# Unread products in front of TensorE's data waits, and a third part turned earlier, in a graph network kernel

## The chip, the cores and the metric

The kernel runs on one core of a Trainium2 chip. The metric is the device time of one execution in microseconds. TensorE is PE in the profile (PEld is its weight load), VectorE is DVE, ScalarE is ACT, GpSimd is POOL and SyncE, which only issues transfers here, is SP.

## The reference

A graph of 50,000 nodes and 50,000 edges, the edges sorted by their destination, goes through four message passing layers; each ends with a layer norm over the 160 features of a node (64 scalars, and 32 vectors of three components). Cut to what matters:

```python
x = _layernorm(x + _L0_gnn_ref(x, node_vec1, edge_attr_3, edge_attr_64, src, dst, ...))  # attention
x = _layernorm(x + _L1_gnn_ref(x, node_vec1, edge_attr_16, edge_attr_4, src, dst, ...))  # mean
x = _layernorm(x + _L2_gnn_ref(x, node_vec1, edge_attr_4, edge_attr_8, ..., src, dst, 16))
x = _layernorm(x + _L3_gnn_ref(x, node_vec1, src, dst, edge_attr_4, edge_attr_64, ...))

# each layer, in short
h = silu(edge_scalars @ fc_w1); w = h @ fc_w2              # weights of an edge
m = combine(w, (x @ lin1)[src], edge_attr)                 # messages, scalars and vectors
agg = segment_sum(m, dst)                                  # sums of a node
y = x @ sc + agg @ lin2                                    # and gates of each layer's own
```

Layer 0 has a two-layer radial network with layer norms, attention logits with a softmax over a node's edges, and a feed-forward part behind it.

## The kernel before

Everything is float32. Nodes and edges are padded to 98 chunks of 512, a chunk being 4 tiles of 128. The program is a row of stages, each over all 98 chunks, with tables in DRAM between them: setup, node_pre (98 to 497 us), edge_logits (600 to 2096), edge_softmax, node_first (2620 to 3858), and then edge_layer and node_layer for the layers 1, 2 and 3.

Within a stage every engine has a program of its own, written with `pipeline(engine, chunks, [(stage, delay), ...])`: in round r the engine executes, in the order of the list, each stage for chunk r - delay. That list is the order of the work. Engines wait on each other only by semaphores (`wait_ge`). A product on PE has two kinds of wait: for its data (an earlier engine's result), and for its bank in PSUM (the reader of the last product in it must be done). A round is one chunk, so all engines of a stage have the same mean round.

The names that matter:

- `turn` (L391) transposes five 128x128 blocks into a bank pair, `mix` (L397, L400) multiplies the turned rows by a layer's weights in ten products.
- edge_logits: PE's stages in order are values of r = 0, roots (`r2`, `r1`), `h1`, `h2`, values of r = 1, two variances, `messages_t` (12 transposes, L1353), weights of r = 0 (L1360), `logits` (4 transposes, L1380), weights of r = 1 (L1360). ACT copies or evaluates each result out of PSUM. POOL issues eight gathers a chunk and takes powers (L1279). DVE makes the messages.
- node_first: PE runs `hidden` (L1759 to L1764), turn and mix of sums, projection (L1739 to L1744), turns and `outputs` (L1777 to L1782).
- edge_layer: PE runs `hidden` (L473), turns of the message parts (L487; two parts in layers 1 and 2, three in layer 3), `sums` (L510), `weights` (L497) and `linear` (L522 to L525). In layer 3 the third part's turn stands between weights and linear. ACT copies (L557 turned, L562 rows, L544 radial).
- node_layer: PE runs `front` (turn of the loaded rows), and for layers 1 and 2 `turn_out`, `back` (mix of the skip part), `mix_out`; for layer 3 only front and back. SP loads indices and rows and stores the normalised rows. POOL gathers the sums (L718) and takes a power (L767). DVE runs `before` (L967 to L973 in layer 3) and `combine` (L1011 to L1018, statistics L739 to L755).

In node layer 3 the banks of `back` alternate (`sc_s` is 2048 + 1024 * slot), but its product also waits for DVE's `combine` two chunks back:

```python
pe.wait_ge(xt_sb.sem, xt_sb.after(s.g + 1))
pe.wait_ge(sum_step.sem, sum_step.after((s.g - 1 + with_e) * sum_steps - with_e * (sum_steps - read)))
pe.wait_ge(pre_step.sem, pre_step.after((s.g - 1) * pre_steps))
```

## Time and profile before

| | us |
|---|---|
| median of 3 runs | 8838.66 (8814.75 to 8842.85) |
| the profiled execution | 8821.47 |
| its span | 8819.7 |
| PE busy | 6072.5 (69%) |
| PE weight load busy | 5115.7 (58%) |
| DVE busy | 6244.2 (71%) |
| ACT busy | 4194.7 (48%) |
| POOL busy | 4731.4 (54%) |

The mean granted TensorE clock is 0.822 of full speed. The profile's page gives the shares over the whole span; since the stages have different limits, they are read stage by stage from the trace. In a timeline a line shows start, duration, engine, line of the program, operation, operands, and in brackets the engine's idle time before it and what ended it. A line of the waits gives an engine and its line, what released it, the sum in us, how many times and the longest.

### The profile page before, as it was taken

The numbers are of one execution on the slowest core, as the hardware profiler recorded it, in microseconds if no ns is written. First come the engines' busy times: TensorE is split into PE (matmuls) and PEld (weight loads), VectorE is DVE, ScalarE is ACT, GpSimd is POOL, SyncE is SP. The second block draws the span as 40 slices with busy tenths as digits, with TensorE's granted clock in tenths as the row PEclk, the third lists the DMA queues.
The fourth block names the chain that finished last, engine by engine and source line by source line (L and its number), as shares of the span: only waits on it lengthen the run. The fifth ranks groups of instructions, "written<-read, shape, count | busy, mean of one in ns | idle before, by whom it ended". The sixth has DMA issues, their size and how long they took to land. (4 is left out here: it accounts for less than half of the span.)

```text
span 8819.7 us, 169625 instructions
## 1 busy us (share of the span) xinstructions
PE 6072.5 (69%) x36496; PEld 5115.7 (58%) x36496; DVE 6244.2 (71%) x20178; ACT 4194.7 (48%) x10003; POOL 4731.4 (54%) x4424
## 2 busy tenths in 40 slices
PE   3767777776657777777776666777666678884444
PEld 3555555555556666656665655666566567774443
DVE  6967777777658887866565775666688878785666
ACT  2544444443325555544444775444466645553333
POOL 3456666664445555545444554445466544445666
PEclk9977777776559999988888887889788899996666
DMA  6732222224753333334444665444466544443444
GB/s 185 242 119 75 75 76 75 77 71 133 205 168 105 108 110 103 106 92 120 116 117 131 198 196 158 116 116 120 122 178 179 172 120 129 128 122 115 128 128 124
DMA packets 774197, 1137.24 MB, mean 129 GB/s; under 512 B 322032, under 2 KB 410038, under 8 KB 773648
## 3 DMA queue, kind: packets, MB, share of 16 engines
q1 hardware_dynamic: 591952, 831.36, 30.2%
q0 software_dynamic: 182144, 304.74, 15.4%
q8 instruction: 37, 0.61, 0.0%
q14 instruction: 64, 0.52, 0.0%
HBM read 667.03 MB, written 472.87 MB: 129 GB/s over the span
## 5 line engine op out<-in xcount | busy, mean ns | idle before, releaser
L718 POOL DMA_INDIRECT agg<-seg_rows,node_idx x1568 | 1530.1, 976 | 1137.2 <-issue 924.4
L457 POOL DMA_INDIRECT erow<-e_rows,ids x1176 | 1220.0, 1037 | 1282.4 <-issue 1176.6
L397 PE MATMUL banks<-w_all,xt 128*128 128x128 f32 (+1 forms) x2352 | 559.7, 375 | 939.8 <-DVE stats L755 424.4
L397 PEld LDWEIGHTS banks<-w_all,xt 128*128 128x128 f32 x2352 | 439.2, 251 | 1027.9 <-issue 999.5
L767 POOL TENSOR_TENSOR stats<-stats,power 128x4 f32<-128x4 f32 (+1 forms) x392 | 524.8, 1339 | 544.6 <-DVE stats L755 341.9
L655 POOL DMA_INDIRECT row_of_dram<-where x392 | 431.7, 1101 | 559.0 <-DMA where<-place_dram 417.9
L487 PE MATMUL banks<-w_all,mid 128*128 128x128 f32 (+1 forms) x2744 | 457.9, 293 | 395.4 <-ACT hid_p L538 355.0
L400 PE MATMUL banks<-w_all,xt 128*128 128x128 f32 x3528 | 658.5, 339 | 0.0
L487 PEld LDWEIGHTS banks<-w_all,mid 128*128 128x128 f32 (+1 forms) x2744 | 327.7, 146 | 524.0 <-ACT hid_p L538 415.7
L400 PEld LDWEIGHTS banks<-w_all,xt 128*128 128x128 f32 x3528 | 620.9, 254 | 0.0
L544 ACT ACTIVATE radial<-banks 128x768 f32<-128x768 f32 (+1 forms) x294 | 248.6, 846 | 650.1 <-PE banks L497 362.1
L523 PE MATMUL banks<-w_all,turned 128*128 128x97 f32 (+1 forms) x2352 | 502.4, 297 | 43.0 <-issue 33.2
L1272 POOL DMA_INDIRECT y<-dst_table,edge_idx x392 | 439.8, 1122 | 119.5 <-issue 119.5
L557 ACT ACTIVATE turned<-banks 128x512 f32<-128x512 f32 (+1 forms) x686 | 409.5, 599 | 195.7 <-PE banks L487 101.6
L562 ACT ACTIVATE rows<-banks 128x772 f32<-128x772 f32 (+1 forms) x294 | 250.0, 850 | 493.7 <-PE banks L525 293.1
L1272 POOL DMA_INDIRECT work<-src_table,edge_idx x392 | 415.7, 1061 | 112.1 <-issue 112.1
L525 PE MATMUL banks<-w_all,turned 128*128 128x96 f32 x2352 | 459.9, 278 | 0.0
L510 PE MATMUL banks<-rows,segs 128*128 128x161 f32 (+1 forms) x2352 | 451.9, 342 | 3.2 <-DVE rows L618 3.2
L359 DVE TENSOR_TENSOR mid<-radial,erow 128x256 f32<-128x256 f32 x294 | 125.6, 427 | 436.0 <-issue 184.6
L523 PEld LDWEIGHTS banks<-w_all,turned 128*128 128x128 f32 x2352 | 375.7, 201 | 99.5 <-issue 89.8
L582 DVE TENSOR_TENSOR segs<-dst_row,ids 128x512 f32<-128x512 int32 x294 | 202.8, 690 | 323.6 <-remote 117.2
L785 ACT ACTIVATE xo<-y,stats 128x64 f32<-128x64 f32 (+1 forms) x1200 | 428.4, 445 | 0.0
(282 smaller groups left out, 18272.0 us busy)
## 6 DMA issues: line engine op xcount, KB each, us to landing
x_rows<-xo SPq DMA_DIRECT2D x294, 324.0 KB
xin<-x_rows SPq DMA_DIRECT2D x294, 324.0 KB
e_rows<-ets SPq DMA_DIRECT2D x294, 322.0 KB
dst_row<-in_dst_flat SPq DMA_DIRECT2D x294, 256.0 KB
xin<-in_x SPq DMA_DIRECT2D x196, 324.0 KB
seg_rows<-res SPq DMA_DIRECT2D x196, 322.0 KB
seg_rows<-res SPq DMA_DIRECT2D x98, 384.0 KB
seg_rows<-res SPq DMA_DIRECT2D x98, 338.0 KB
```

The source lines that it names most:

```text
L397: pe.matmul(flat[:, to + k * cols:to + (k + 1) * cols], of[:, k * P:(k + 1) * P], W(w_s), start=True, stop=True)
L400: last = pe.matmul(flat[:, to + 2 * cols + k * P:to + 2 * cols + (k + 1) * P], of[:, (2 + k) * P:(3 + k) * P], W(w_v), start=True, stop=True)
L457: pool.indirect_dma_start(erow[s.quad][:, t, 0:EROW], None, table, bass.IndirectOffsetOnAxis(ids[s.quad][:, t:t + 1], 0),).then_inc(edges_ ...
L487: last = pe.transpose(psum[0:n, b, t * P:(t + 1) * P], mid[s.slot][:, t, k * P:k * P + n], ident)
L510: last = pe.matmul(tiled(6, cols)[:, t], segs[s.quad][:, t, :], rows[s.slot][:, t, 0:cols], start=True, stop=True)
L523: pe.matmul(to[:, t, 0:v_at + C1], mid_t[:, 0, cut], W(f"la{layer}"), start=not crossed, stop=True, skip_group_check=crossed)
L525: last = pe.matmul(to[:, t, v_at + C1:cols + C1], mid_t[:, 1, cut], W(f"lb{layer}"), start=not crossed, stop=True, skip_group_check=crossed)
L655: pool.indirect_dma_start(row_of_dram, bass.IndirectOffsetOnAxis(where[b][:, at + t:at + t + 1], 0), where[b][:, at + TILES + t:at + TILES ...
L718: pool.indirect_dma_start(agg[s.quad][:, t, 0:SUM_COLS[layer]], None, seg_rows[layer], bass.IndirectOffsetOnAxis(node_idx[s.slot][:, t, 0: ...
L767: pool.tensor_tensor(st[:, at + n:at + 2 * n], st[:, at:at + n], power[:, 0:n], ALU.pow) \
L785: last = act.activation(to, of if at == 0 else of.rearrange("p (i c) -> p i c", i=3), ACT.Identity, bias=st[:, 40 + t:41 + t], scale=st[:, ...
L1272: pool.indirect_dma_start(to[s.slot][:, t, :], None, table, bass.IndirectOffsetOnAxis(idx[s.slot][:, first + t:first + t + 1], 0),).then_i ...
```

## The change

A helper `spare(pe, b, times)` issues products of the identity with 512 columns of the weights into bank b, which nobody reads. It is put between the wait for the bank and the wait for the data, so in several places the two waits change their order. In the logits: two in `messages_t`, two before the weights of r = 0, one before the values of r = 0, one in `logits` (six a round). In node_first: one in `hidden`, one in `outputs`. In edge layers 1 and 2: one in `linear`. In node layers 1 and 2: two in `turn_out`, two in `mix_out`. In node layer 3: five in `back`, where the wait for `sum_step` is dropped. That makes 588 + 196 + 196 + 784 + 490 = 2254 such products.

In edge layer 3 the third part is turned (PE) and copied (ACT) right after the other two. In edge layers the bank's wait of `linear` comes first. In node layers SP issues its stores one round earlier.

```diff
+        def spare(pe, b, times):
+
+            for _ in range(times):
+                pe.matmul(bank(b), ident, w_all[:, 0:512], start=True, stop=True)
...
                     def linear(s):
 
+                        pe.wait_ge(linear_sb.sem, linear_sb.after(s.g))
+                        if not crossed:
+                            spare(pe, 4, 1)
                         pe.wait_ge(part_sb.sem, part_sb.after(parts * (s.g + 1)))
-                        pe.wait_ge(linear_sb.sem, linear_sb.after(s.g))
...
-                        (hidden, 0), (lambda s: turn_part(s, 0), 2), (lambda s: turn_part(s, 1), 2), (sums, 4), (weights, 0),
-                        *[(lambda s: turn_part(s, 2), 2)][:parts - 2], (linear, 2)])
+                        (hidden, 0), (lambda s: turn_part(s, 0), 2), (lambda s: turn_part(s, 1), 2),
+                        *[(lambda s: turn_part(s, 2), 2)][:parts - 2], (sums, 4), (weights, 0), (linear, 2)])
...
-                        (hidden, 0), (lambda s: copy_part(s, 0), 2), (lambda s: copy_part(s, 1), 2), (weights, 0),
-                        *[(lambda s: copy_part(s, 2), 2)][:parts - 2], (sums, 4), *[(wrap, 0)][:crossed], (linear, 2)])
+                        (hidden, 0), (lambda s: copy_part(s, 0), 2), (lambda s: copy_part(s, 1), 2),
+                        *[(lambda s: copy_part(s, 2), 2)][:parts - 2], (weights, 0), (sums, 4), *[(wrap, 0)][:crossed], (linear, 2)])
...
-        def turn_out(pe, s, to):
+        def turn_out(pe, s, to, times=0):
             precompute(pe, norm_sb.after(s.g + 1), xt3_sb.after(s.g))
             pe.wait_ge(ready.sem, 1)
+            pe.wait_ge(xt3_sb.sem, xt3_sb.after(s.g))
+            spare(pe, to // 512, times)
             pe.wait_ge(norm_sb.sem, norm_sb.after(s.g + 1))
-            pe.wait_ge(xt3_sb.sem, xt3_sb.after(s.g))
...
-        def mix_out(pe, s, layer, to):
+        def mix_out(pe, s, layer, to, times=0):
             precompute(pe, xt3_sb.after(s.g + 1), ets_sb.after(s.g))
             pe.wait_ge(ready.sem, 1)
+            pe.wait_ge(ets_sb.sem, ets_sb.after(s.g))
+            spare(pe, to // 512, times)
             pe.wait_ge(xt3_sb.sem, xt3_sb.after(s.g + 1))
-            pe.wait_ge(ets_sb.sem, ets_sb.after(s.g))
...
-                        pipeline(sp, chunks, [loads, (lambda s: store_nodes(sp, s, x_rows[layer + 1]), 6),
-                                              (lambda s: store_e(sp, s, layer + 1), 7)])
+                        pipeline(sp, chunks, [loads, (lambda s: store_nodes(sp, s, x_rows[layer + 1]), 5),
+                                              (lambda s: store_e(sp, s, layer + 1), 6)])
                     else:
-                        pipeline(sp, chunks, [loads, (store_out, 6)])
+                        pipeline(sp, chunks, [loads, (store_out, 5)])
...
                     def back(s):
 
+                        if not with_e:
+                            pe.wait_ge(pre_step.sem, pre_step.after((s.g - 1) * pre_steps))
+                            spare(pe, sc_s(s) // 512, 5)
                         pe.wait_ge(xt_sb.sem, xt_sb.after(s.g + 1))
-                        pe.wait_ge(sum_step.sem, sum_step.after((s.g - 1 + with_e) * sum_steps - with_e * (sum_steps - read)))
+                        if with_e:
+                            pe.wait_ge(sum_step.sem, sum_step.after(s.g * sum_steps - (sum_steps - read)))
...
-                        stages = [(front, 0), (lambda s: turn_out(pe, s, TURN2), 4), (back, 0),
-                                  (lambda s: mix_out(pe, s, layer + 1, 3072), 4)]
+                        stages = [(front, 0), (lambda s: turn_out(pe, s, TURN2, 2), 4), (back, 0),
+                                  (lambda s: mix_out(pe, s, layer + 1, 3072, 2), 4)]
...
                     def messages_t(s):
+                        pe.wait_ge(agg_sb.sem, agg_sb.after(3 * s.g - 1))
+                        spare(pe, 0, 2)
                         pe.wait_ge(mid_step.sem, mid_step.after((s.g + 1) * steps))
...
                     def weights(s, r):
+                        pe.wait_ge(w_sb.sem, w_sb.after(2 * s.g + r))
                         if r == 0:
+                            spare(pe, 7, 2)
                             pe.wait_ge(silu2_sb.sem, silu2_sb.after(s.g + 1))
-                        pe.wait_ge(w_sb.sem, w_sb.after(2 * s.g + r))
...
                     def values(s, r):
+                        pe.wait_ge(val_sb.sem, val_sb.after(2 * s.g + r))
                         if r == 0:
+                            spare(pe, 3, 1)
                             pe.wait_ge(agg_sb.sem, agg_sb.after(3 * s.g + 3))
-                        pe.wait_ge(val_sb.sem, val_sb.after(2 * s.g + r))
...
                     def logits(s):
                         precompute(pe, leaky_step.after(s.g * leaky_steps + 3), logit_sb.after(s.g))
                         pe.wait_ge(ready.sem, 1)
+                        pe.wait_ge(logit_sb.sem, logit_sb.after(s.g))
+                        spare(pe, 2, 1)
                         pe.wait_ge(leaky_step.sem, leaky_step.after(s.g * leaky_steps + 3))
-                        pe.wait_ge(logit_sb.sem, logit_sb.after(s.g))
...
                     def hidden(s):
 
+                        pe.wait_ge(hidden_step.sem, hidden_step.after(s.g * hidden_steps))
+                        spare(pe, 4, 1)
                         pe.wait_ge(xt2_sb.sem, xt2_sb.after(s.g + 1))
-                        pe.wait_ge(hidden_step.sem, hidden_step.after(s.g * hidden_steps))
...
                         pe.wait_ge(ets_sb.sem, ets_sb.after(s.g - 2))
+                        pe.wait_ge(mid_step.sem, read)
+                        spare(pe, 2, 1)
                         pe.wait_ge(gate_sb.sem, gate_sb.after(s.g + 1))
                         pe.wait_ge(hidden_step.sem, hidden_step.after((s.g + 1) * hidden_steps))
-                        pe.wait_ge(mid_step.sem, read)
```

## Rows read from the trace of the kernel before

**Rows 1.** Windows by stage: length, busy PE, PEld, DVE, ACT, POOL, PEclk, DMA, GB/s.
```profile
600.00:2096.00 1496.00, 1125.22 (x5663) 840.14 (x5664) 1083.94 (x2352) 675.22 (x1879) 966.86 (x835) 0.75 0.28 74
2620.00:3858.00 1238.00, 948.88 (x6764) 795.30 (x6764) 1019.10 (x4529) 657.04 (x1701) 637.57 (x574) 0.96 0.37 105
3905.00:4711.00 806.00, 612.15 (x4014) 525.70 (x4016) 486.85 (x1257) 343.74 (x574) 396.37 (x391) 0.85 0.44 116
4753.00:5421.00 668.00, 427.05 (x2848) 390.89 (x2849) 497.86 (x2033) 464.48 (x1321) 370.55 (x387) 0.85 0.66 193
5450.00:6250.00 800.00, 597.08 (x4008) 511.97 (x4009) 485.56 (x1256) 344.34 (x575) 398.22 (x391) 0.88 0.44 115
6295.00:7032.00 737.00, 461.03 (x2829) 431.87 (x2829) 639.20 (x2791) 490.01 (x1411) 479.49 (x482) 0.80 0.61 174
7064.00:7931.00 867.00, 709.09 (x5162) 601.41 (x5158) 688.98 (x1646) 449.04 (x767) 420.11 (x390) 0.98 0.45 125
7981.00:8805.00 824.00, 379.31 (x1450) 344.21 (x1450) 504.84 (x1635) 283.58 (x671) 531.49 (x482) 0.62 0.44 127
```

**Rows 2.** Timeline of node layer 3, 8400 to 8420 us.
```profile
8401.35 1.64 PE L397 MATMUL banks<-w_all,xt 128*128 128x192 f32 x4 [4.81 <-DVE stats L755]
...
8404.07 1.27 PE L391 MATMUL banks<-w_all,xin 128*128 128x128 f32 x5
...
8409.25 1.02 POOL L718 DMA_INDIRECT agg<-seg_rows,node_idx  x1 [2.02 <-issue]
...
8409.84 1.64 PE L397 MATMUL banks<-w_all,xt 128*128 128x192 f32 x4 [4.50 <-DVE stats L755]
...
8412.80 0.56 DVE L967 TENSOR_TENSOR aux<-banks,agg 128x384 f32<-128x384 f32 x1 [3.03 <-PE banks L400]
...
8414.05 1.66 POOL L767 TENSOR_TENSOR stats<-stats,power 128x4 f32<-128x4 f32 x1
```

**Rows 3.** Waits, 8200 to 8600 us (node layer 3).
```profile
ACT work L901 <- DMA out<-work: 163.2, 47, 4.0
```

**Rows 4.** Timeline of edge layer 3, 7500 to 7520 us.
```profile
7504.59 0.92 ACT L544 ACTIVATE radial<-banks 128x896 f32<-128x896 f32 x1 [1.77 <-PE banks L497]
7505.41 0.58 ACT L557 ACTIVATE turned<-banks 96x512 f32<-96x512 f32 x1
...
7506.12 0.46 PE L522 MATMUL banks<-w_all,turned 96*128 96x96 f32 x2 [1.10 <-ACT turned L557]
```

**Rows 5.** Timeline of the logits, 1466 to 1481 us, PE and DVE.
```profile
1469.41 1.01 PE L1360 MATMUL banks<-w_all,u 128*128 128x448 f32 x2 [1.27 <-ACT u L1410]
...
1471.71 1.02 PE L1360 MATMUL banks<-w_all,u 128*128 128x448 f32 x2 [0.84 <-DVE radial L1517]
...
1474.29 0.60 PE L1327 MATMUL banks<-scal_e,w_all 128*128 128x256 f32 x2
1474.73 0.59 PE L1335 MATMUL banks<-u,w_all 128*128 128x256 f32 x2
...
1468.66 0.42 DVE L1496 SCALAR_TENSOR_TENSOR leaky_x<-alpha_th,alpha 128x256 f32<-128x256 f32 x1
...
1480.33 0.42 DVE L1496 SCALAR_TENSOR_TENSOR leaky_x<-alpha_th,alpha 128x256 f32<-128x256 f32 x1
```

**Rows 6.** Waits, 600 to 1900 us (logits).
```profile
ACT alpha_th L1426 <- remote: 139.1, 34, 7.0
```

**Rows 7.** Timeline of node_first, 3000 to 3026 us.
```profile
3015.46 0.70 PE L1759 MATMUL banks<-xt,w_all 128*128 128x256 f32 x2 [0.35 <-ACT xt L1800]
```

**Rows 8.** Edge layer 1: waits 4050 to 4650, timeline, and a 3 us window.
```profile
PE banks L487 <- ACT hid_p L538: 125.6, 60, 6.4
...
4188.17 1.12 PE L487 MATMUL banks<-w_all,mid 128*128 128x128 f32 x4 [2.93 <-ACT hid_p L538]
...
4188.00:4191.00 3.00, 2.83 (x12) 2.84 (x12) 0.98 (x2) 1.20 (x3) 2.02 (x3) 0.50 0.39 119
```

**Rows 9.** Waits, 4760 to 5400 us (node layer 1).
```profile
DVE xo L759 <- DMA x_rows<-xo: 31.2, 46, 1.5
```

## The prediction, made before the changed kernel was run

> **What bounds the kernel now.** I read the windows first, one per stage: for each its length, the busy time of every engine and the mean granted TensorE clock (PEclk) [rows 1]. The stages run one after the other, and the change touches all eight listed ones and none of the others. Each has 98 rounds (one chunk of 512), so a length divided by 98 is a round, and what a round gains or loses counts 98 times. The reader is to see three things. No engine is busy all the time in any stage; each is a ring of engines waiting for one another. The last node stage (7981 to 8805) is the loosest: PE is busy 379 of 824 us, DVE 505, POOL 531, and the clock is 0.62. And the logits (600 to 2096) have the clock at 0.75, the node_first stage (2620 to 3858) at 0.96, edge layer 3 (7064 to 7931) at 0.98. Where the clock is full already, a product that nobody reads can only cost.
>
> Second view: the timeline of one round of each stage, to see what PE waits for at the very place where something is inserted or moved [rows 2, 4, 5, 7]. Third: the waits, for the stages that are irregular [rows 3, 6, 8].
>
> **The price of a spare product.** The trace of before has no 128x512 product on PE. The nearest is the 128x256 one in the logits: a pair of L1327 starts at 1474.29 and the next line at 1474.73, so 256 columns take 0.44 us at full clock and 512 take 0.88 [rows 5]. From above: the 448-column pair of L1360 is 1.01 us long including its tail, which scales to 1.15 [rows 5]. I take 0.88, because spares stand in a row and their tails overlap. At half clock I estimate twice that, 1.76. Its floor is zero, where PE would have idled. The spare writes a bank that is free and reads weights that never change, so it adds no wait of its own; everything behind it on PE's queue is later by what it doesn't hide.
>
> **Node layer 3: wait removed, five spares, store one round earlier.** Now mixing starts when DVE has done its last statistics (PE L397 at 8409.84 idle 4.50 us for DVE stats L755), runs 2.96 us at half clock until 8412.80, and DVE L967 has idled 3.03 us for it [rows 2]. PE and DVE work in turns: a round is 8.49 us (8401.35 to 8409.84). The change takes the wait for DVE's sums away; the mix needs only the turned rows and the free half of the banks, which alternate. Then DVE's 3.03 us of idling go, which leaves a DVE round of 5.5. What is late next: POOL. From its first gather at 8409.25 to the end of its power at 8415.71 (8414.05+1.66) are 6.46 us [rows 2], plus about 0.2 to the next gather: 6.65. PE with five spares at full clock: 4.4, plus the mix 1.48 and the turn L391 0.64 (half of their 2.96 and 1.27 at half clock), 6.5. ACT's normalising waits for the store of the output (163.2 us over 47 rounds, 3.5 each [rows 3]); that wait lies beside other work now and would become the bound, but the store goes out a round earlier, which takes it away. On SP's queue the store moves ahead of one round's two loads and delays these by its issue; their data is needed two rounds later, so that costs nothing while SP idles. I take 6.9 a round: (8.49-6.9) x 98 = **-155 us**, between -100 (7.5, PE and POOL collide) and -180 (6.65).
>
> **Edge layer 3: third part turned before the weights.** Each round PE idles 1.10 us at L522 for ACT's copy L557 of the third part, because that copy stands behind ACT L544 (0.92 us from 7504.59, the copy from 7505.41) [rows 4]. Moved, the turn and its copy lie beside the sums and weights products (2.35 us), and the linear products follow the weights directly. What goes is the idle 1.10; what comes back is some 0.3, since ACT's L544 is now next to the linear products' results. No spare is added here. PE is 709 of 867 us busy, DVE 689 [rows 1], so PE's round of 8.85 may fall to about 8.1 before DVE (7.0) matters. **-73 us** (0.75 x 98), between 0 and -100.
>
> **Node_first: two spares.** A closed ring through PE and ACT at nearly full clock. The hidden layer's spare stands where PE idles 0.35 us at L1759 for ACT xt [rows 7]; the other stands before the output products, which start with no idle time. So 2 x 0.88 - 0.35 = 1.41 a round, 138 us. The missing 0.04 of the clock would come back: worth some 20 us. **+115 us**, from +60 to +150.
>
> **Logits: six spares.** Take a round at full clock: DVE L1496 starts at 1468.66 and 1480.33, 11.67 us apart [rows 5]. The mean is 15.27 [rows 1]; the difference is the half clock and stalls. In the fast round the two spares before the first L1360 fall on its idle 1.27 (+0.49), the one in front of the logits' transposes falls on the 0.84 that the second L1360 waits for DVE (+0.04), and three have no cover (+2.64): 14.84 if the clock stays full. PE then has 5.3 + 8.6 (its busy 11.5 a round times the clock of 0.75) = 13.9 of work in it. ACT's stalls for a store or DVE (139.1 us over some 85 rounds, 1.6 each [rows 6]) are partly swallowed by the longer ring; I keep 0.35. 15.2 a round: **-10 us**, from -137 (13.9) to +130 (clock only 0.85).
>
> **Edge layers 1 and 2: one spare each, before the linear products.** PE runs into these without idling in a smooth round. But the smooth round is rare: PE waits for ACT hid_p 125.6 us in 600, once for 2.93 us, and the 3 us window behind that wait has PEclk 0.50 [rows 8]. Uncovered, 0.88 x 196 = 172; the slack of rounds that stall takes part, the clock (0.85 and 0.88 [rows 1]) some more. If the clock came back whole I'd have about -1.1 + 0.9 - 0.2. I take +0.2 a round: **+40 us**, from -80 to +172.
>
> **Node layers 1 and 2: four spares a round, both stores one round earlier.** PE is busy 4.4 and 4.7 of 6.8 and 7.5 us, at clocks 0.85 and 0.80 [rows 1]. At full clock the work is about 3.5, with spares 7.0. Layer 1 thus becomes PE bound near its present round; its DVE waits for the store of the rows (0.7 us, 46 times [rows 9]) go with the earlier store, but in the ring that gives little. **+25 us**, from -15 to +70. Layer 2 has DVE at 6.5 of 7.5, and idle PE hides the spares: **+5 us**, from -20 to +40.
>
> **Sum.** -155 - 73 + 115 - 10 + 40 + 25 + 5 = **-53 us** on the profiled execution's 8821.5 (span 8819.7 and 1.8 around it), 8768. That execution is 0.2% below the median 8838.7; moved onto it: **8785 us**.
>
> **A rule weighed.** The window right behind a PE wait of 2.93 us has a granted clock of 0.50, its lower level of 1.2 GHz [rows 8]. The Trainium skill, "TensorE: Matmul & The Clock Gate", What's actually happening, says that "the default state is throttled, and activity releases the throttle": filling waits with products would keep the fast clock. The trace agrees where gaps are long. The same page, HAM oscillation, prices throttled time at half of it; for the logits alone, with half of 1496 us at the low clock, that estimate would be 374 us at most. What stands against so large a gain in the rows are the products themselves, 5.3 us a round, and the 11.67 of the fast round.
>
> **Rivals.**
> (a) *The forecast*: full clock returned, spares mostly uncovered in the logits and node_first, a large gain in node layer 3. 8785, own range 8700 to 8870.
> (b) *Slower: the spares don't lift the clock in the logits and edge layers.* The stalls there come from stores and gathers, and a spare standing before such a wait runs out long before 3 to 6 us of it are over, so the low clock follows as before. Then the logits' spares are paid in part at 1.76: at PEclk 0.85 or less +1.3 a round (+130), edges +0.6 x 196 (+120); with the rest -155 - 73 + 115 + 25 + 5: +167, **9005**. It decides from a logits round over 16 us. For it: 34 long ACT stalls [rows 6]. Against it: PE's share of busy time in the logits would rise from 0.75 to over 0.9.
> (c) *Faster: the spares pay.* The slack hides them and the clock does the rest: logits at PE's 13.9 (-137), edges -0.4 x 196 (-80), node layers 1 and 2 zero, node_first +80: with -155 and -73, -365, **8475**. Against it: the three logits spares and those in node_first stand where PE does not idle [rows 5, 7]. The Trainium skill, "TensorE: Matmul & The Clock Gate", HAM oscillation, with its price for throttled time, speaks for this case.
> (d) *Node layer 3 stays cold or doesn't gain*: five spares at 1.76 and the mix at 2.96 and turn 1.2 make 13 us a round, +440: **9380**. Against: PE would be over 90% busy.
> (e) *Node layer 3's gain is eaten* by the gathers or by the store (7.9 a round, -60) and edge layer 3 gives -30: **8920**.
>
> **How the numbers follow.** (a) 0.5, (b) 0.17, (c) 0.13, (d) 0.03, (e) 0.17. The uncertainty inside (a) is mostly logits (-127 to +140 about the value), edges (-120 to +132) and node_first. I count 0.33 of (a) as faster by over 0.3% (26 us; about what a measurement here tells from no change), 0.12 as within it and 0.05 slower; (c) is faster; (b), (d) are slower; of (e) 0.04 is within it, 0.03 faster, 0.10 slower. That gives faster 0.49, same 0.16, slower 0.35. The range leaves out (d), the far part of (b) and most of (c): 8610 to 8980.
>
> **What would show each step right or wrong.** Node layer 3: PE L397 no longer follows DVE L755, clock near 1, rounds about 6.9, POOL with idle time under 0.4; a clock of 0.5 there is (d). Edge layer 3: no idle before L522 (as numbered before), rounds of 8.1. Node_first: rounds of 13.8, the clock unchanged. Logits: clock above 0.95 and rounds of about 15.2; below 0.9 with rounds over 16 is (b), 14 is (c). Edge layers 1 and 2: 8.4 a round. Node layers 1 and 2: PE busy over 90% at full clock. The prediction is wrong if the length of the stages outside these eight moves, or if a spare costs more than 1.0 us at full clock.

## The result, and the profile after

The changed kernel takes 8958.4 us (median of 3 runs, 8954.9 to 8976.0) where the kernel before takes 8838.7: ratio 1.0148, 95% interval 1.0114 to 1.0183. It is slower by 1.5%. The forecast was 8785. The profiled execution took 8954.9 us, its span is 8953.1, and its mean TensorE clock is 0.919 where it was 0.822.

The same windows by stage as in [rows 1], of the changed kernel (length, then busy time of PE, PEld, DVE, ACT, POOL, then PEclk, DMA share, GB/s):

```profile
600.00:2245.00 1645.00, 1456.64 (x6805) 967.33 (x6804) 1082.29 (x2353) 670.13 (x1882) 938.02 (x835) 0.90 0.25 68
2768.00:4056.00 1288.00, 1056.60 (x7150) 834.01 (x7151) 1017.61 (x4530) 659.52 (x1701) 639.35 (x574) 0.99 0.35 101
4104.00:4902.00 798.00, 656.29 (x4204) 527.45 (x4206) 490.53 (x1258) 343.50 (x574) 397.37 (x390) 0.92 0.44 117
4946.00:5697.00 751.00, 672.15 (x3601) 469.35 (x3602) 497.60 (x2036) 471.22 (x1323) 371.39 (x387) 0.96 0.59 172
5729.00:6535.00 806.00, 655.62 (x4200) 525.86 (x4196) 489.36 (x1257) 344.38 (x574) 398.37 (x390) 0.92 0.43 114
6580.00:7345.00 765.00, 672.34 (x3576) 464.59 (x3577) 636.43 (x2792) 485.11 (x1408) 486.02 (x483) 0.97 0.57 168
7381.00:8223.00 842.00, 699.83 (x5175) 606.71 (x5175) 690.54 (x1646) 451.10 (x769) 420.20 (x391) 0.97 0.46 129
8274.00:8939.00 665.00, 613.55 (x2418) 367.31 (x2416) 511.05 (x1635) 283.94 (x671) 515.57 (x480) 0.99 0.53 156
```

DVE, ACT and POOL are busy as long as before in every stage, within 3%; PE is busy longer, at a faster clock, everywhere but in edge layer 3. The clock is 0.90 or above in all eight stages. The time is another matter: node layer 3 (last row) is 159 us shorter, edge layer 3 25 us, and the logits are 149 us longer, node layer 1 83, node_first 50, node layer 2 28, with edge layers 1 and 2 at -8 and +6.

From here on a round is the time from a stage's first to its last round, measured at one DVE operation that runs once a round, divided by 97. The column "forecast x 98" is as the prediction gave it, from its own bases (15.27 in the logits, 12.63 in node_first, 8.85 in edge layer 3: a window divided by 98).

| stage | before | forecast | after | forecast x 98 | measured x 98 |
|---|---|---|---|---|---|
| logits | 15.47 | 15.2 | 16.99 | -10 | +149 |
| node_first | 12.76 | 13.8 | 13.28 | +115 | +50 |
| edge layers 1, 2 | 8.31, 8.25 | +0.2 | 8.23, 8.31 | +40 | -2 |
| edge layer 3 | 8.94 | 8.1 | 8.68 | -73 | -26 |
| node layer 1 | 6.89 | 7.1 | 7.74 | +25 | +83 |
| node layer 2 | 7.60 | 7.6 | 7.89 | +5 | +28 |
| node layer 3 | 8.50 | 6.9 | 6.86 | -155 | -161 |
| sum | | | | -53 | +121 |

The stages that the change doesn't touch agree within 0.01 us a round (4.11 and 4.12 in node_pre, 4.76 and 4.75 in the softmax), so a stage is a good ruler. The sum misses by 174 us, and 159 of them are the logits. The other misses are not small (-65, -42, +47, +58, +23 and -6), but they nearly cancel, which is luck.

A round of the logits, timeline of PE and ACT, 1100 to 1140 us (L391 is now the spare product; x4 is two of them):

```profile
1116.57 0.28 ACT L1444 ACTIVATE alpha_th<-banks 128x128 f32<-128x128 f32 x1 [3.33 <-remote]
...
1117.51 0.49 PE L1386 MATMUL banks<-w_all,mid_t 97*128 97x128 f32 x2 [1.39 <-ACT products L1447]
...
1119.77 3.60 PE L391 MATMUL banks<-w_all 128*128 128x512 f32 x4
1123.16 1.14 PE L1368 MATMUL banks<-w_all,mid 128*97 128x128 f32 x8
...
1125.05 1.88 PE L391 MATMUL banks<-w_all 128*128 128x512 f32 x4
1126.76 0.92 PE L1376 MATMUL banks<-w_all,u 128*128 128x448 f32 x2
```

Two things are to be seen. At full clock two spares take 1.71 us from start to start (1125.05 to 1126.76), 0.86 each, as the forecast had it with 0.88. And the pair in front of the messages' transposes takes 3.39 (1119.77 to 1123.16): ACT has come late by 3.33 us, PE has idled 1.39 for it, and while the pair runs the granted clock is 0.50, which is the lower of its two levels, 1.2 GHz:

```profile
1120.00:1123.00 3.00, 3.00 (x4) 1.05 (x4) 2.90 (x10) 0.00 (x0) 1.72 (x2) 0.50 0.03 4
```

So here the products without cover are the ones that pay the half clock.

### The profile page after: what moved, and what is told of

Same layout as the page of the kernel before. It is cut to its first block and busy times, and to the rows that moved or that the text cites. A ratio compares the mean times of both kernels' runs of the same rounds, so it can differ in the third digit from the quotient of the medians.

```text
span 8953.1 us, 178351 instructions
## 1 busy us (share of the span) xinstructions
PE 7331.6 (82%) x41004; PEld 5445.8 (61%) x41004; DVE 6251.2 (70%) x20178; ACT 4195.8 (47%) x10003; POOL 4701.9 (53%) x4424
## 3 DMA queue, kind: packets, MB, share of 16 engines
q0 software_dynamic: 182144, 304.74, 15.2%
## 5 line engine op out<-in xcount | busy, mean ns | idle before, releaser
L391 PE MATMUL banks<-w_all 128*128 128x512 f32 x4508 | 2310.7, 632 | 2.7 <-ACT lg L1452 1.5
L725 POOL DMA_INDIRECT agg<-seg_rows,node_idx x1568 | 1573.5, 1004 | 1100.2 <-issue 890.8
L391 PEld LDWEIGHTS banks<-w_all 128*128 128x128 f32 x4508 | 814.7, 201 | 634.0 <-issue 633.9
L774 POOL TENSOR_TENSOR stats<-stats,power 128x4 f32<-128x4 f32 (+1 forms) x392 | 476.9, 1217 | 586.7 <-DVE stats L762 369.3
L492 PE MATMUL banks<-w_all,mid 128*128 128x128 f32 (+1 forms) x2744 | 429.4, 287 | 423.4 <-ACT hid_p L545 370.9
L402 PEld LDWEIGHTS banks<-w_all,xt 128*128 128x128 f32 x2352 | 346.2, 195 | 360.7 <-issue 274.6
L402 PE MATMUL banks<-w_all,xt 128*128 128x128 f32 (+1 forms) x2352 | 401.8, 294 | 177.8 <-ACT xt L893 44.3
L405 PE MATMUL banks<-w_all,xt 128*128 128x128 f32 x3528 | 503.3, 280 | 0.0
L530 PE MATMUL banks<-w_all,turned 128*128 128x97 f32 (+1 forms) x2352 | 462.6, 279 | 8.5 <-issue 8.5
L405 PEld LDWEIGHTS banks<-w_all,xt 128*128 128x128 f32 x3528 | 459.1, 197 | 0.0
L815 ACT ACTIVATE xt<-banks 128x640 f32<-128x640 f32 x294 | 206.7, 703 | 508.5 <-PE banks L396 323.6
```

What stands on the lines that cost most here:

```text
L391: pe.matmul(bank(b), ident, w_all[:, 0:512], start=True, stop=True)
L402: pe.matmul(flat[:, to + k * cols:to + (k + 1) * cols], of[:, k * P:(k + 1) * P], W(w_s), start=True, stop=True)
L405: last = pe.matmul(flat[:, to + 2 * cols + k * P:to + 2 * cols + (k + 1) * P], of[:, (2 + k) * P:(3 + k) * P], W(w_v), start=True, stop=True)
L492: last = pe.transpose(psum[0:n, b, t * P:(t + 1) * P], mid[s.slot][:, t, k * P:k * P + n], ident)
L530: pe.matmul(to[:, t, 0:v_at + C1], mid_t[:, 0, cut], W(f"la{layer}"), start=not crossed, stop=True, skip_group_check=crossed)
L725: pool.indirect_dma_start(agg[s.quad][:, t, 0:SUM_COLS[layer]], None, seg_rows[layer], bass.IndirectOffsetOnAxis(node_idx[s.slot][:, t, 0: ...
```

## The experiments

The stages run one after the other and don't overlap, so one kernel can try something else in each of them. The totals belong to the kernel, the rounds to the stage. Runs were on several chips, and the kernel before was not alike on them: 8855, 8864 and 8729 us on chips called A here, 7872, 7879 and 7867 on chips called B. Each chip was met in one session, so what is called a kind of chip may as well belong to the time or the machine. Rounds are compared on chips of one kind, and each round below is from one trace; on chips A, stages left alone differ between traces by 0.1 to 0.3, so smaller differences say nothing there. A second trace of the kernel before, on another chip A, repeats the first: 15.51, 12.73, 8.22, 8.21, 6.91, 7.62 and 8.49; only edge layer 3 had 9.56 instead of 8.94.

**1. Without any spare product** (chip A). All `spare` calls removed, the rest of the change kept.

> The changed kernel without any of its 2254 spare products; the other edits (order of waits, third part earlier, stores a round earlier, the dropped wait in node layer 3) stay. Theory 1 (the products carry the loss): the logits go back to 15.3 us a round (about 1500 us), node_first to 12.8, so these two lose what they gained in time, together about 200 us; node layer 3, whose mix would be at half clock again, stands at 7.5 to 8.5 a round. Theory 2 (the earlier stores hold up SyncE's queue in node layers 1 and 2): those two stages stay at 7.7 and 7.9 a round although their products are gone; by theory 1 they return to 6.9 and 7.6. In all 8700 to 8780 by theory 1, 8800 by theory 2.

8657.8 us, ratio 0.9794 (0.9745 to 0.9843); on another chip A 8682.0, ratio 0.9771 (0.9731 to 0.9811). Rounds: logits 15.32, node_first 12.94, edge layers 8.13, 8.26, 8.66, node layers 7.19, 7.62, 6.75. Theory 1 holds for the whole: the 2254 products turn a gain of about 2% into a loss of 1.5% (on one and the same chip, runs 9 and 10 below, a gain of 2.3% into a loss of 1.1%). Node layer 3 surprised: its window without products,

```profile
7975.00:8629.00 654.00, 370.87 (x1450) 321.18 (x1450) 510.47 (x1634) 283.75 (x671) 514.45 (x482) 0.61 0.53 159
```

shows a clock of 0.61, as before the change, and is still the shortest. Dropping the wait gives the whole gain; the 490 products there add nothing to it. Node layer 1 at 7.19 for 6.89 says that theory 2 has a part too.

**2. Spare products only** (chip A). Stores, third part and the wait in node layer 3 as before.

> The kernel before with all spare products, and nothing else: old places of the stores, old order of the third part, and the wait on the sums kept in node layer 3, behind the five products. Theory 1: node layers 1 and 2 at 7.7 and 7.9 a round as in the changed kernel; theory 2: at 6.9 and 7.6, since the stores are where they were. Node layer 3: if the gain is the dropped wait, 8.0 to 8.5 a round; if it is the clock (the mix then takes 1.5 instead of 3.0 us between DVE's turns), about 6.9 to 7.1, as in the changed kernel. Logits at 17.0, node_first at 13.3, edge layer 3 at 8.9.

8975.5 us, ratio 1.0150 (1.0101 to 1.0199). Logits 17.15, node_first 13.22, edge layers 8.22, 8.24, 8.99, node layers 7.04, 7.82, 7.12. With the wait kept, node layer 3 gets to 7.12 by the clock alone. Timeline of that stage:

```profile
8509.26 0.17 DVE L762 TENSOR_SCALAR stats<-stats 128x4 f32<-128x4 f32 x1
...
8509.49 0.92 PE L402 MATMUL banks<-w_all,xt 128*128 128x192 f32 x4 [0.74 <-DVE stats L762]
8510.24 0.83 PE L405 MATMUL banks<-w_all,xt 128*128 128x128 f32 x6
...
8511.11 0.56 DVE L979 TENSOR_TENSOR aux<-banks,agg 128x384 f32<-128x384 f32 x1 [1.61 <-PE banks L405]
```

The mix begins right behind DVE's statistics as in [rows 2], but takes 1.6 instead of 3.0 us. So the clock and the wait are two ways to nearly the same gain, and they don't add up: behind both stands POOL, whose 2.02 us of idle time before a round's first gather [rows 2] are 0.19 in the changed kernel, where the mix waits for nothing:

```profile
8611.37 0.81 PE L402 MATMUL banks<-w_all,xt 128*128 128x192 f32 x4
...
8611.70 1.02 POOL L725 DMA_INDIRECT agg<-seg_rows,node_idx  x1 [0.19 <-issue]
```

In node layer 1 the products alone cost 0.15 and the earlier stores alone 0.30 against the first trace, where both together cost 0.85. These are traces of two chips; runs 8 to 10 below have all three on one.

**3. and 4. One place each** (chip A).

> Part of the products, one place in each stage; old stores and old order of the third part. Logits with only the product before the values: it stands where TensorE waits for ScalarE's products, so 15.0 to 15.5 a round if covered, as theory 1 has it. Node_first with only the hidden layer's product: 12.8 to 13.0 (covered 0.35 of 0.88). Edge layers 1 and 2 with their product: 8.2. Node layers 1 and 2 with two products in turn_out only, old stores: 6.9 and 7.6 if SyncE's queue is what costs; 7.3 and 7.8 if the products do. Node layer 3 with the wait dropped, five products and the old place of the store: 6.9 if the store's place doesn't matter, 8 or more if ScalarE's wait for the store binds.

> The other places. Logits with only the two products in front of the transposes of the messages: they stand on the ring vector messages, transposes, weights, and come right behind TensorE's long wait, so at half clock and full price: 17 a round if this place carries the loss, 15.5 if the number of products does. Node_first with only the product before the outputs: 13.3. Edge layers 1 and 2 without product: 8.2. Edge layer 3 with TensorE's order changed and ScalarE's not: the copy is still behind the radial one, 8.9; if the order on ScalarE is what made the new wait for hid_p, 8.4. Node layers 1 and 2 with two products in mix_out only, new stores: 7.6. Node layer 3 with two products instead of five: 6.9 if the clock stays up, 8 if it falls.

Run 3: 8742.9 us (ratio 0.9880, 0.9818 to 0.9941); logits 15.77, node_first 13.07, edge layers 1 and 2 8.26, 8.28, node layers 6.98, 7.64, 6.82. Run 4: 9135.0 us (1.0323, 1.0258 to 1.0388); logits 17.28, node_first 12.71, edge layer 3 11.39, node layers 7.22, 7.80, 6.75. (In run 4 the stores of node layers 1 and 2 stand in their old places, not in the new ones as its expectation says, so its 7.22 is two products in mix_out alone.) The two products in front of the messages' transposes cost 1.8 to 2.0 a round on their own, at least their full price of 1.7. The store's place doesn't matter in node layer 3 (6.82). And edge layer 3 punishes half a reordering: with PE turning the third part early but ACT copying it late, PE idles 2.51 us at the linear products instead of 1.10, and a round takes 11.39:

```profile
7814.35 0.67 PE L527 MATMUL banks<-w_all,turned 96*128 96x96 f32 x2 [2.51 <-ACT turned L562]
```

**5. to 7. Four in the logits; moved and doubled; store first** (chip B).

> Four products in the logits (two before the first weights, one before the values, one before the logits' transposes), none in front of the messages' transposes; no products anywhere else; stores of all node layers back in their old place; the third part earlier and the dropped wait of node layer 3 stay. Theory 1, by place: only what stands between the messages of VectorE and their transposes is on the ring, so the logits are at 15.2 to 15.8 a round, as with one product. Theory 1, by number: two thirds of 1.6, so 16.3. Node layers 1 and 2: 6.9 and 7.6. Node layer 3 without products and with the store in its old place: 6.7 if the store's place doesn't matter, above 7.5 if it does. In all about 8650.

> Logits with the same six products, but the two from the messages' transposes put with the one before the values: by place about 15.8 a round, by number 17.0. Edge layers 1 and 2 with two products instead of one: 8.3 if they are hidden, 9.1 if each costs 0.88. Node layers 1 and 2 with all their products, the nodes' store a round earlier and the store of the gathered table in its old place: 7.7 in layer 1 if the nodes' store is what meets the products badly, 7.0 if it is the table's. Node layer 3: wait on the sums kept, store early, no products: 8.4, since mixing and combining still take turns at half clock. Node_first and edge layer 3 as changed: 13.2 and 8.7.

> Logits as before, without products, but SyncE issues the store of the values ahead of two loads instead of behind them: if ScalarE's long waits before alpha are for that store, 14.5 or less a round; if they are not, 15.4 as before. Node_first with two products before the outputs and none in the hidden layer: 13.3 if each costs as on a ring, 12.7 if the product there is covered. Edge layers all as before: 8.3, 8.3, 8.9. Node layers 1 and 2 without products, nodes' store early, table's store in its old place: 6.9 if only the table's store matters, 7.2 if it is the nodes'. Node layer 3 with ten products instead of five, wait dropped: TensorE becomes the bound at 10 x 0.88 + 2.1 = 10.9 a round.

7548.0 us (ratio 0.9582, 0.9566 to 0.9598), 8293.9 (1.0534) and 8131.4 (1.0328). On these chips the rounds of a stage hardly vary, and a product costs what it costs: edge layers 1 and 2 are at 5.76 and 5.75 with none and 7.40 and 7.42 with two, node layer 3 at 10.45 with ten. Edge layer 3 goes from 8.67 to 7.61 by the reordering. The logits were the surprise: 12.72 without products, 12.19 with four, 13.47 with the six of which three stand before the values. Windows of the logits without products (run 17 below) and with four:

```profile
597.00:1831.00 1234.00, 994.79 (x5669) 780.48 (x5668) 1076.64 (x2362) 687.69 (x1886) 957.81 (x839) 0.85 0.33 90
```

```profile
597.00:1780.00 1183.00, 1138.01 (x6430) 799.48 (x6430) 1065.17 (x2357) 692.38 (x1883) 935.22 (x838) 1.00 0.35 95
```

Here four products (3.4 us of PE) bring the clock from 0.85 to 1.00 and the stage is 51 us shorter. PE is then busy 1138 of 1183 us, so further ones have little to hide in: the fifth and sixth add 1.3 together. Node layer 3 with its wait kept, an earlier store and no products stays at 8.43. Node layer 1 is at 6.26 with old stores and 5.95 with the nodes' store earlier: on this chip that store helps; with all products and the nodes' store earlier (run 6) it is at 6.66. Node_first with two products before the outputs takes 12.91.

**8. to 11. Before, after, no products, and what run 5 pointed to, side by side** (chip A).

> The kernel before, unchanged, with a trace of its own, because the kernel before took 8855 us on the chip of the first four experiments and 7872 on that of the next three: this gives its stages on the chip of this call. Where the chip is like the second, I expect the edge layers at 5.8, 5.8 and 8.7 a round (as without products there), the logits at 12.7 or less, node_first at 12.1, node layer 3 at 8.4; like the first, the stages of the trace already shown.

> The changed kernel, unchanged, beside it. If the chip has no long stalls, the products have nothing to hide in. Theory 1: logits 15, node_first 12.9, edge layers 1 and 2 at 5.75 + 0.88 = 6.6, edge layer 3 at 7.6, node layer 1 at 6.8, node layer 3 at 6.9: about +230 + 80 + 170 - 105 + 70 - 150, so 8150 where the kernel before takes 7872, a loss of 3.5% rather than 1.5%. Rival: the clock gives back more where nothing stalls, and the loss is 1.5% as on the first chip.

> The changed kernel without any spare product, as the first experiment, beside the other two on the same chip. Logits as in the kernel before, node_first and edge layers 1 and 2 too, edge layer 3 at 7.6, node layer 1 at 6.3 or less, node layer 3 at 6.75: 7872 - 105 - 165 = 7600 on a chip without stalls, 8660 on one with them.

> What the runs so far point to: no products except four in the logits (not in front of the messages' transposes), third part earlier, wait dropped in node layer 3, the nodes' store of layers 1 and 2 a round earlier and the other stores in their old places. If the four products return the clock at no cost, the logits are at 12.2 on a chip without stalls, below the kernel without products by 0.2 a round or more, and the whole is at 7530; on a chip with stalls 15.4 in the logits and 8640.

8873.4, 8981.8 (ratio 1.0109, 1.0070 to 1.0147), 8682.0 (0.9771) and 8910.5 us (1.0050, 1.0021 to 1.0079). Node layer 1 has 6.91, 7.49, 7.41 and 7.41: on this chip the earlier stores cost 0.50 and the products 0.08 more, which is within the scatter. My candidate fell: the four products that had won 0.5 us a round in the logits on chip B cost 2.3 here, 17.73 for 15.40, more than all six (17.31). The window of the four:

```profile
597.00:2310.00 1713.00, 1461.43 (x6406) 1065.15 (x6405) 1092.37 (x2355) 677.64 (x1882) 959.45 (x837) 0.79 0.24 65
```

And the same stage with all six (run 9) and with none (run 10), on that chip:

```profile
597.00:2276.00 1679.00, 1475.19 (x6822) 979.09 (x6822) 1086.85 (x2363) 672.68 (x1893) 933.97 (x837) 0.89 0.24 66
597.00:2090.00 1493.00, 1120.42 (x5681) 835.43 (x5680) 1088.79 (x2363) 676.93 (x1885) 977.35 (x839) 0.75 0.27 74
```

The clock is 0.75 with none, 0.79 with four and 0.89 with six. With four, PE is busy 341 us longer than with none, and 392 products at 0.86 are 337: nothing of the clock comes back. With six it is 355 for 506, so 151 come back. Of PE's idle time the four fill 121 us and the six 169. These two differences are why four cost more than six here; why the clock rises with the one set and not with the other no run shows. "By place", as I had it after run 4, is thus refuted as the whole story: the two in front of the transposes are not needed for the loss.

**12. to 15. The remaining splits** (chip A).

> The changed kernel without spare products and with the stores of node layers 1 and 2 in their old places; third part earlier, wait dropped and store earlier in node layer 3 stay. If the earlier stores cost by themselves in layer 1 (7.2 to 7.4 a round without products against 6.9 before), this is the fastest of the versions: ratio 0.974 on a chip with stalls.

> Logits with only the two products before the first weights (they fall on the 1.27 us that TensorE waits for ScalarE there): 15.6 a round if that wait covers them, 17 if it doesn't. Edge layers 1 and 2 with two products: 8.3 to 8.5 if the stalls hide them. Node layers 1 and 2 without products, only the table's store early: 6.9 if the nodes' store is what costs, 7.3 if it is the table's. Node layer 3 without wait and products, old store: 6.75.

> Logits without products and with the store of the values ahead of two loads: unchanged at 15.4 if ScalarE's long waits have nothing to do with it. Node_first with two products before the outputs: 13.3. Node layers 1 and 2 with two products in turn_out, old stores: 7.0 and 7.7. Node layer 3 with the wait kept, no products, store early: 8.5.

> The changed kernel with every spare product cut from 512 to 128 columns, so each costs 0.22 us at full clock. If the loss is their duration on the ring, three quarters of it go: logits 15.3 + 0.4 to 0.6 = 15.8 a round, node_first 12.8, node layer 1 7.3, and the clock falls back to about 0.8 in the logits; node layer 3 stays at 6.8 since the dropped wait carries it. In all about 8740, below the kernel before. If it is their number (issue, semaphores), the logits stay at 17.

8554.7 us (ratio 0.9797, 0.9749 to 0.9845), 8615.7 (0.9879), 8748.9 (1.0010) and 8619.0 (0.9873, 0.9825 to 0.9921). Logits: 15.10 without products, 15.52 with the two that stand on the wait of [rows 5], 14.87 with the store of the values first, 16.12 with all six at 128 columns. So the covered pair costs 0.4 and not its 1.7, and three quarters less of each product take half of the loss away (+1.0 for +1.9). The columns carry at least that half. The short products bring the clock to 0.82 only, and all that they last (6 x 0.22, an estimate from 0.86 for 512 columns) is 1.3; how the other half splits between this and their number no run shows. Edge layers 1 and 2 with two products: 8.17 and 8.27, nothing. Node layer 1: 6.78 with both stores old, 6.85 with only the table's store earlier; run 11, with only the nodes' store earlier, had 7.41 on the chip where run 8 had 6.91. It is the nodes' store. Run 14 has node_first at 13.21 with two products before the outputs, node layer 1 at 7.00 with two in turn_out and old stores, and node layer 3 at 8.43 with its wait kept, no products and the store early. In the traces the nodes' earlier store makes the short rounds shorter and the long ones longer: with it and without products (run 10) a quarter of the rounds take 5.74 us or less and a tenth 10.2 or more, in the kernel before (run 8) 6.14 and 8.1.

**16. to 18. A candidate, its control, and the changed kernel again** (chips B).

> The version that the runs point to: no products except two of 128 columns in node_first, the values' store first on SyncE in the logits, stores of node layers 1 and 2 in their old places, third part earlier, wait dropped and store earlier in node layer 3. Against s1: -0.2 to -0.5 a round in the logits (the store had 14.87 for 15.10 there) and -0.4 in node_first (12.40 for 12.82), so 40 to 80 us less, a ratio of 0.972 on a chip with stalls. If these were chance, 0.980.

> The same as s1, beside the candidate on the same chip: ratio 0.980 to the kernel before.

> The changed kernel once more. On a chip without stalls (kernel before at about 7875) theory 1 has the logits at 13.5 to 14.5 a round for 12.9 without products, node_first 12.9 for 12.1, edge layers 1 and 2 at 6.6 for 5.75, node layer 1 at 6.8 for 6.2, edge layer 3 and node layer 3 gaining 105 and 160: about 8000 to 8050, a ratio of 1.02. On one with stalls 1.011 to 1.015 as measured twice.

7600.7 (ratio 0.9646, 0.9633 to 0.9659), 7603.4 (0.9654, 0.9641 to 0.9668) and 7974.0 us (1.0130, 1.0113 to 1.0147). The store of the values first and the small products in node_first give nothing there (12.74 for 12.72, 12.04 for 12.05); on chips A their gains rest on single traces and stay open. The changed kernel has on chip B: logits 13.49, node_first 12.91 (12.05 without products), edge layers 6.57, 6.57 (5.75, 5.74) and 7.61, node layers 6.68 (6.18), 7.56, 6.78. Rounds of edge layer 1, PE, without (run 17) and with its product:

```profile
3705.32 0.66 PE L492 MATMUL banks<-w_all,mid 128*128 128x128 f32 x4 [0.28 <-ACT hid_p L543]
...
3711.06 0.66 PE L492 MATMUL banks<-w_all,mid 128*128 128x128 f32 x4 [0.28 <-ACT hid_p L543]
```

```profile
3906.43 0.66 PE L492 MATMUL banks<-w_all,mid 128*128 128x128 f32 x4 [0.28 <-ACT hid_p L545]
...
3908.97 1.12 PE L391 MATMUL banks<-w_all 128*128 128x512 f32 x2
...
3913.03 0.66 PE L492 MATMUL banks<-w_all,mid 128*128 128x128 f32 x4 [0.28 <-ACT hid_p L545]
```

5.74 against 6.60: the product is wholly on the ring, with the clock already full, and 0.86 is its price.

The version without products and with old stores in node layers 1 and 2 is ahead of the kernel before on both kinds of chip, by 2.0% on A and 3.5% on B, and so ahead of the changed kernel, which is behind by 1.1 to 1.5% on both.

## Why the prediction was wrong

**The price of a product** was right: 0.86 for the 0.88 that [rows 5] gave.

**Node layer 3** was right, time and mechanism: -161 for -155, PE's mix no longer behind DVE, POOL next. POOL's idle time is 0.19 before a round's first gather, as the sign for this step had asked. What I had attached to it, that at the low clock the round would be 13 us, counts the five products in: without them it is 6.75 at a clock of 0.61. In my sum I should have asked what the stage does with the wait dropped and nothing added.

**The logits** are the step that failed, +149 for -10. The term of the sum that failed is "I keep 0.35". A fast round of 11.67 stood against a mean of 15.27, so stalls and half clock were 3.6 us a round, and I let the products and the longer ring take all but 0.35 of them. They took next to nothing of it. On chip B, where the clock is 1.00 and nothing stalls, the round with six products is 13.49; on chips A its mean is 16.99 and 17.31, so 3.5 to 3.8 are still there. The fast round itself, 14.84, was set too high by 1.35, and that was luck: it hid a part of the miss. What is made good of the products' time, on either kind of chip, is made good inside the fast round and not out of the rest. (Rounds of 14.98 do occur in the trace of after, but only a tenth of its rounds are below 15.04, and half take 17.8 or more.)

PE's time in this stage, as an account, shows where the six products went. They are 588 x 0.86 = 506 us. On chip A (runs 9 and 10, windows above) the clock gives 151 back, 169 fill idle time, and the stage is 186 longer. On chip B (run 18, window below, against run 17) it is 223, 208 and 75, and PE is busy 98% of the stage:

```profile
597.00:1906.00 1309.00, 1277.52 (x6815) 877.43 (x6816) 1074.11 (x2360) 678.99 (x1887) 988.76 (x838) 1.00 0.31 85
```

The forecast of -10 asked for all 506 to be made good, which they are on neither.

Behind the term stood a wrong reading. [rows 6] has 1.6 us a round of ACT waits marked "remote", which means that no instruction was found beside the signal that ended them. I took them for waits for a store or for DVE. Putting that store first changed the round by 0.2 on one chip A (14.87 for 15.10, one trace each) and by nothing on B. The signals recorded in the traces say what they were: all 32 such waits of the trace of after, and all 34 of the trace of before, ended with the semaphore that PE's own products for the values raise. One of them:

```profile
1131.49 0.39 PE L1388 MATMUL banks<-w_all,mid_t 128*128 128x64 f32 x2
...
1134.54 0.28 ACT L1444 ACTIVATE alpha_th<-banks 128x128 f32<-128x128 f32 x1 [4.33 <-remote]
```

The last of these products ends at 1131.87 by its record, its signal comes at 1134.52, and ACT starts at once. This is the rule on chips A. Over the whole kernel before, 1392 of 4583 recorded signals of PE come more than 0.3 us behind the recorded end of the product that raises them; of the changed kernel on chip B (run 18), none of 5201, the latest 0.03 us behind. In the logits the latest signal of a round is late by 3.0 us on average before and by 2.4 after. So the delay sits at PE, it is 0.6 smaller in the longer ring, and the waits stand in the trace of after almost as before (waits, 600 to 1900 us, and the same of the changed kernel on chip B, where none is "remote"):

```profile
ACT alpha_th L1444 <- PE banks L1388: 129.6, 91, 5.3
ACT alpha_th L1444 <- remote: 119.4, 32, 5.7
```

```profile
ACT alpha_th L1444 <- PE banks L1388: 149.3, 88, 3.8
```

Whether PE finishes late or only signals late, and what delays it, stays open.

**Rival (b)** came nearest. Its deciding point, a logits round over 16 us, was met and its sign was right, but its mechanism only in part: the clock did rise (0.90, above its 0.85) and fell again behind stalls like the one at 1116; but these are no waits for stores or gathers, as it had them. Its edge layers (+120) were wrong, and its 9005 is 47 us too high.

**Edge layers 1 and 2**: -2 for +40, well inside the bounds. The slack of stalled rounds hides one product and even two (8.17, 8.27 in run 13). Here the delay of PE's signals does shrink as products come in: the latest of a round is late by 2.2 and 2.5 us in the kernel before, 1.2 and 1.6 with one product, 0.8 and 1.1 with two. Why it gives way here and hardly in the logits is open. On chip B, where nothing stalls, the upper bound of my range nearly came true: 0.82 and 0.83 a round for 0.88.

**Edge layer 3**: -26 for -73 against this trace, -85 against the other trace of the kernel before on a chip A, -104 on chip B. The mechanism was right: on chip B it gains more than I had allowed. On chips A PE's idle time before the linear products is gone and partly back at the turns, where it waits for ACT hid_p, behind ACT's copy of the rows (timeline of after; 0.39 us stood there before):

```profile
7808.05 1.13 PE L492 MATMUL banks<-w_all,mid 128*128 128x128 f32 x8 [1.19 <-ACT hid_p L545]
```

I had allowed 0.3 for what comes back; it is 0.8 in this round, and 0.33 for PE's wait there on chip B. The late signals are part of the difference: in this stage 17 of 602 before (76 of 582 in the other trace) and 195 of 622 after.

**Node_first**: +50 for +115, below my range. On chip B it is +0.87 a round (85 us), where I had 1.41 less the clock. The mis-sized term is the cover of the hidden layer's product: without products PE idles 0.53 to 0.62 there on chip B (run 17), where I had 0.35, which gives 2 x 0.86 - 0.6 = 1.1; what covers the last 0.2 is open. It is no matter where the two stand: both before the outputs give 12.91 as well (run 7). On chips A another 0.35 a round goes into rounds that stalled anyway: the median round is 0.9 longer there too (12.46 to 13.36), but a twentieth of the rounds took 16.65 or more before and 13.72 after.

**Node layer 1**: +83 for +25. What was mis-sized is the nodes' earlier store: I costed it as a wait that goes away, and it adds 0.3 to 0.5 a round on chips A, while on chip B it takes 0.2 to 0.3 away. The products cost 0.15 (run 2) and 0.08 (run 9 against run 10) there and 0.71 on chip B, where nothing stalls (6.66 in run 6 for 5.95 in run 7). That both together cost more than their sum (0.85 for 0.45) is so against the first trace only; on the one chip A that had all three traces it is 0.50 and 0.08. On SyncE the earlier store also is a wait for ACT's normalising that the next round's loads stand behind; that this is how it costs is argued from the order of SyncE's queue, not shown. **Node layer 2**: +28 for +5, in range; there the stores cost nothing (7.62 without products) and the products 0.2 to 0.35 on chips A.

**The rule weighed**: the products do keep TensorE longer at its 2.4 GHz level, 0.919 for 0.822 over the span, as the Trainium skill, "TensorE: Matmul & The Clock Gate", What's actually happening, has it ("activity releases the throttle"). The trace agrees. What it was worth was to be read elsewhere: in node layer 3, with the wait dropped, the stage takes 6.75 a round at 0.61 and 6.86 at 0.99; with the wait kept, so that the mix is on the ring, 8.50 falls to 7.12. In this kernel the clock was worth something only where PE's duration was on the ring.

## What to carry to other kernels

Before adding work to keep an engine's clock up, take a round at full clock in the trace and ask what each addition costs there, and then what the low clock costs in the others; a faster clock on an engine that isn't on the ring buys nothing. When a wait is dropped and filler added in one edit, cost the dropped wait alone: here it was the whole gain. And split a mean round into its fast round and the rest, and don't let new work pay for itself out of the rest before you know what it waits for: here such a rest took up two products in edge layers 1 and 2 and hardly any of six in the logits.

## What the runs showed of the hardware that was not expected

The same kernel takes 8729 to 8864 us on some chips and 7867 to 7879 on others, 11 to 13% apart. Executions on one chip of the first kind spread over 0.9 to 1.2%, on one of the second over 0.1 to 0.3%. What sets the two apart in the traces is PE: on the first kind a third of its signals come late, by up to several us, on the second none, while the signals of DVE come within 0.3 us on both but for ten or fewer of over 10,000. In the logits ACT then starts some operations 1 to 4 us behind the recorded end of the product that they read. SyncE's issue instructions sometimes take 0.70 instead of 0.35 us, as in this timeline of node layer 1 in the changed kernel; that is more frequent on the first kind (some 250 of 4686 for 100 of 4686) but not its mark:

```profile
5302.84 0.70 SPq L716 DMA_DIRECT2D xin<-x_rows  x1
5303.72 0.36 SPq L734 DMA_DIRECT2D x_rows<-xo  x1
```

Edge layers 1 and 2 are hit hardest, 8.2 us a round against 5.75. What causes it, and whether it belongs to the chip, no run shows. For a decision like this one it matters: the four products in the logits are worth -4% of that stage on one kind and cost 15% of it on the other, so a variant tuned on one chip has to be timed on both.
